# A recommendation tower on one core: the order in which TensorE turns the gathered embeddings is changed

## What is computed

```python
e = jnp.stack([tbl_0[ids[:, 0]], ..., tbl_26[ids[:, 26]]], axis=1)       # 2048 x 27 x 128
interactions = jnp.einsum('bfd,bgd->bfg', e, e)
flat_interactions = interactions[:, _TRIU_I, _TRIU_J]                     # 351 pairs, i < j
z = jnp.concatenate([e.reshape(B, -1), flat_interactions], axis=1)
h = jnp.concatenate([z, dense_ctx], axis=1)                               # 2048 x 3823
h = jnp.maximum(h @ W_top1 + b_top1, 0.0)                                 # 512
h = jnp.maximum(h @ W_top2 + b_top2, 0.0)                                 # 256
y = h @ W_top3
```

## Time and profile before

| | |
|---|---|
| median of three runs | 576.74 us |
| span of the profiled execution | 708.0 us |
| mean granted TensorE clock in it | 0.908 |
| PE busy | 574.9 us, 81% of the span |
| POOL busy | 416.2 us, 59% |
| DVE busy, ACT busy | 347.6 us, 232.3 us |

### The profile page before, as it was taken

How to read it: one execution, slowest core, us unless ns; L and a number is a source line. 1 busy time by engine, 2 the same in 40 slices (tenths; PEclk the granted TensorE clock), 3 DMA queues, 4 the chain that set the end, 5 groups by cost and what they waited for, 6 DMA issues and landing times.

```text
span 708.0 us, 7882 instructions
## 1 busy us (share of the span) xinstructions
PE 574.9 (81%) x2578; PEld 504.6 (71%) x2578; DVE 347.6 (49%) x1140; ACT 232.3 (33%) x703; POOL 416.2 (59%) x450
## 2 busy tenths in 40 slices
PE   2606688989889898959959896897968979698898
PEld 1505577868778787948848795786857868697786
DVE  4305462819264563808337281554707355372755
ACT  4204423324251513315232331514315161323441
POOL 6775565666666565665746667365664666556001
PEclk9956899989989998989989899799987999989999
DMA  6613411111111111111111111011110111111000
GB/s 211 217 52 110 131 45 44 46 46 44 45 45 50 41 49 41 48 45 39 47 29 50 44 42 52 27 49 42 46 52 26 49 41 49 42 41 46 12 1 1
DMA packets 19581, 37.84 MB, mean 53 GB/s; under 512 B 7780, under 2 KB 8804, under 8 KB 19540
## 3 DMA queue, kind: packets, MB, share of 16 engines
q0 software_dynamic: 13824, 28.34, 15.1%
q1 hardware_dynamic: 5716, 8.99, 4.0%
HBM read 37.30 MB, written 0.01 MB: 53 GB/s over the span
## 4 chain that ended last, share of the span: by engine, by line
PE 59%; another core or an unknown queue 20%; DVE 8%; issue 6%; ACT 5%; DMA 1%; SPq 0%; ACTq 0%; DVEq 0%
PE ps_acc L298 12%; PE ps_acc L299 11%; PE ps_acc L300 11%; PE ps_gram L323 10%; DVE g_buf L666 6%; PE ps_acc L356 6%; PE ps_t L269 5%; PE ps_gram L400 3%; ACT g_buf L582 2%; DVE emb_x L645 1%; DMA g_buf<-in_W_top 1%; ACT emb_x L534 1%; ACT h_t L571 1%; PE ps_gram L352 1%
## 5 line engine op out<-in xcount | busy, mean ns | idle before, releaser
L242 POOL DMA_INDIRECT emb<-in_tbl,idx x405 | 385.8, 953 | 233.4 <-issue 109.4
L298 PE MATMUL ps_acc<-w_hi,emb_x 128*128 128x512 f32 x432 | 211.1, 489 | 28.7 <-DVE emb_x L645 26.6
L645 DVE TENSOR_TENSOR emb_x<-ps_t,emb_x 128x512 fp32r<-128x512 f32 (+1 forms) x111 | 73.9, 667 | 249.6 <-ACT emb_x L534 165.2
L299 PE MATMUL ps_acc<-w_lo,emb_x 128*128 128x512 f32 x432 | 182.7, 423 | 0.0
L300 PE MATMUL ps_acc<-w_hi,emb_x 128*128 128x512 f32 x432 | 181.0, 419 | 0.0
L666 DVE COPY g_buf<-ps_gram 32x112 f32<-32x112 f32 x480 | 129.8, 270 | 93.6 <-PE ps_gram L323 63.1
L323 PE MATMUL ps_gram<-emb_x 128*128 128x224 f32 x480 | 99.5, 335 | 79.2 <-DVE emb_x L645 41.2
L298 PEld LDWEIGHTS ps_acc<-w_hi,emb_x 128*128 128x128 f32 x432 | 131.9, 305 | 35.3 <-DVE emb_x L645 28.0
L323 PEld LDWEIGHTS ps_gram<-emb_x 128*128 128x128 f32 x480 | 83.4, 231 | 102.0 <-DVE emb_x L645 45.1
L582 ACT ACTIVATE g_buf<-ps_gram 32x112 f32<-32x112 f32 x480 | 122.2, 255 | 99.0 <-PE ps_gram L323 64.8
L534 ACT ACTIVATE emb_x<-ps_t 128x512 fp32r<-128x512 f32 (+1 forms) x111 | 63.1, 583 | 272.7 <-PE ps_t L269 137.4
(11 more groups left out here) (61 smaller groups left out, 163.2 us busy)
## 6 DMA issues: line engine op xcount, KB each, us to landing
g_buf<-in_W_top SPq DMA_DIRECT2D x27, 256.0 KB
emb<-in_tbl,idx POOLq DMA_INDIRECT x405
w_cols<-in_W_top SPq DMA_DIRECT2D x1, 512.0 KB
w<-in_W_top SPq DMA_DIRECT2D x1, 512.0 KB
emb<-in_tbl,idx_first POOLq DMA_INDIRECT x27
w_cols<-in_W_top SPq DMA_DIRECT2D x1, 222.0 KB
idx<-in_ids SPq DMA_DIRECT2D x1, 216.0 KB, 4.9
ctx_rows<-in_dense_ctx SPq DMA_DIRECT2D x4, 32.0 KB
```

Source lines behind the costliest of these rows:

```text
L242: pool.indirect_dma_start(out=emb[:, f * D:(f + 1) * D], out_offset=None, in_=tables[f], in_offset=bass.IndirectOffsetOnAxis(ap=rows, axis ...
L298: pe.matmul(acc, emb_part(0, f), w_hi[:, f, :], start=(f == 0), stop=False)
L299: pe.matmul(acc, emb_part(0, f), w_lo[:, f, :], start=False, stop=False)
L645: dve.tensor_tensor(group_part(1, g), turned_bank(n, g), group_part(0, g).bitcast(fp32), ALU.subtract).then_inc(s_emb_lo, 1)
```

## The change

TensorE visits the turns in four places a tile. Groups 2 and 3 are turned one behind the other after the products of group 0; groups 4 and 5 together with the columns after those of group 2; group 6 behind the columns' product; h1 and groups 0 and 1 of the next tile behind unit 11. The two tables that were left for behind the second layer are now multiplied between the units. ScalarE's and VectorE's orders follow: ScalarE copies the columns behind group 5, relu and h1 stand later; VectorE makes the low part of the next tile's group 0 ahead of its last emptying, and that of group 1 ahead of the big transpose, and adds and packs in one piece behind group 3. The last tile's order is as before, but for its first two low parts.

```diff
--- before.py
+++ after.py
@@ -440,7 +440,7 @@
 
 
 
-            BEFORE_UNIT = [2, 0, 0, 2, 0, 0, 1, 0, 0, 1, 0, 0, 1, 0, 0, 0]
+            BEFORE_UNIT = [3, 0, 0, 2, 0, 0, 2, 0, 0, 2, 0, 0, 2, 0, 0, 0]
             assert len(BEFORE_UNIT) == UNITS and sum(BEFORE_UNIT) <= NF - 4 * GF
 
             pe.wait_ge(s_ident, 1)
@@ -449,35 +449,30 @@
             for t in range(TILES - 1):
                 multiply_group(t, 0)
                 turn_group(t, 2)
+                turn_group(t, 3)
                 multiply_group(t, 1)
-                turn_group(t, 3)
                 multiply_group(t, 2)
+                turn_group(t, 4)
+                turn_group(t, 5)
                 if t > 0:
                     turn_columns(t - 1)
-                turn_group(t, 4)
+                multiply_group(t, 3)
                 if t > 0:
                     multiply_columns(t - 1)
-                multiply_group(t, 3)
-                turn_group(t, 5)
-                if t > 0:
-                    turn_h1(t - 1)
+                turn_group(t, 6)
                 f = 4 * GF
-                for _ in range(GF if t == 0 else 2):
-                    multiply(t, f)
-                    f += 1
-                turn_group(t, 6)
                 for k in range(UNITS):
                     for _ in range(min(BEFORE_UNIT[k], NF - f)):
                         multiply(t, f)
                         f += 1
                     gram_unit(t, k)
-                    if k in (8, 14):
-                        turn_group(t + 1, (k - 8) // 6)
+                    if k == 11:
+                        if t > 0:
+                            turn_h1(t - 1)
+                        turn_group(t + 1, 0)
+                        turn_group(t + 1, 1)
                 if t > 0:
                     layer_2(t - 1)
-                while f < NF:
-                    multiply(t, f)
-                    f += 1
 
 
 
@@ -609,14 +604,14 @@
                         for c in GROUPS[g]:
                             split_weights(c)
                     split_group(t, g)
-                    if t > 0 and g == 3:
+                    if t > 0 and g == 5:
                         take_columns(t - 1)
-                    if t > 0 and g == 4:
+                    if t > 0 and g == 6:
                         relu_h1(t - 1)
-                    if t > 0 and g == 5:
-                        take_h1(t - 1)
                 for k in range(0, UNITS, 2):
                     take_blocks(t, k)
+                    if t > 0 and k == 10:
+                        take_h1(t - 1)
             t = TILES - 1
             for g in range(5):
                 split_group(t, g)
@@ -737,22 +732,22 @@
                     if t == 0:
                         for c in GROUPS[g]:
                             split_weights(c)
-                    split_group(t, g)
+                    if t == 0 or g > 1:
+                        split_group(t, g)
                     if t > 0:
-                        if g == 0:
+                        if g == 1:
                             turn_blocks(t - 1)
-                        if g == 1:
+                        if g == 3:
                             add_parts(t - 1)
-                            pack_pairs(t - 1, 0, 10)
-                        if g == 2:
-                            pack_pairs(t - 1, 10, NF - 1)
+                            pack_pairs(t - 1, 0, NF - 1)
                             if t > 1:
                                 layer_3(t - 2)
                 for k in range(1, UNITS, 2):
+                    if k == UNITS - 1:
+                        split_group(t + 1, 0)
                     take_blocks(t, k)
+                split_group(t + 1, 1)
             t = TILES - 1
-            split_group(t, 0)
-            split_group(t, 1)
             turn_blocks(t - 1)
             split_group(t, 2)
             layer_3(t - 2)
```

## The result

The changed kernel took 580.03 us (median of 4 runs, 579.27 to 581.5), the kernel before beside it 577.37 (4 runs): ratio 1.0057, 95% interval 1.0034 to 1.0079. It is slower by 0.6%; no change had been forecast.

The account below looks back on a forecast made before the run. TensorE was taken to bound the kernel, 34.13 us a tile, just ahead of GpSimd's 33.7. + 4.0 at the start, - 4.3 in 13 tiles and + 0.3 at the end gave 576.7 us, range 574 to 580 (8 in 10: 571 to 585).

Parts of the forecast that it names:

- The late signals: Kernel before's first profile: some 142 of 708 us are waits of an unknown queue, belonging to that execution only.
- whatever the others do: GpSimd's gathers: 27 x 1.249 = 33.7 us a tile, independent of the other engines.
- the check by which I came to 34.13: Kernel before: 75.2 to tile 1's units, 13 tiles of 34.0, 57.8 to the end: 575.0; median 576.74 gives 34.13.
- unit 15: TensorE waits for ScalarE to empty unit 12's bank: new wait of 0.95 us a tile.
- the first product: Next tile's first product waits for group 0's low part: new wait of 0.6 us.
- the columns' turn: TensorE waits for VectorE's queue, summed to end at 25.2, after turns 4 and 5 at 24.85: new wait 0.35 us.
- The start: Tile 1: group 5's early turn waits some 3 us for gathers; units start at 79.2, not 75.2, 4.0 us behind.
- It may not run faster than 33.7 a tile either: Changed kernel's tiles: the gathers' rate of 33.7 us is the floor, below the 33.8 forecast for TensorE.
- The end: From unit 0 of tile 14 to the last tile's first turn: + 0.3 us.
- The late start isn't regained: Slower rival: group 5's turn ahead of group 3 costs 4.0 us; 581, or 584 if tiles grow by 0.2; chance 0.22.
- The tiles gain more: Faster rival: tiles save more than forecast, 575.4 at the gathers' floor, 569.5 without it, together some 572; chance 0.26.
- The clock falls: Slower rival: twelve turns between unit 11 and the next product lower TensorE's clock; 587 to 609 us; chance 0.10.

Follow-up runs that it names:

- the second experiment: Both kernels without the product of high embeddings by low weights: kernel before 573.72 us, ratio 0.9934; changed kernel 579.81 us, ratio 1.0040.
- second profile: Trace of the kernel before, unchanged, run again without late signals: span 576.6 us; timed 577.11 us, ratio 0.9994.

## Why the prediction was wrong

**Where TensorE and the gathers stood.** Right in kind: TensorE's order sets the pace of the kernel before, in tiles of 33.94 (I used 34.13), and the gathers could go a little faster (33.72 where almost nothing holds them, by the second experiment; I had 33.7). The late signals did belong to the profiled execution. But the pace of the gathers was wrong: they don't run at their 33.7 "whatever the others do" even here, but come at 33.94, held here and there by VectorE, and TensorE doesn't notice. And three errors of the check by which I came to 34.13 cancelled out, which was luck: tile 1's units come at 80.54, not 75.2; a tile is 0.19 shorter, 2.5 us in 13; and the end from tile 14 on is 54.8, not 57.8, which I had read from the disturbed trace.

**The tile's own work.** I took 33.8 for TensorE in the new order. Alone it needs 33.3 (without the addition) to 33.45 (group 5 late). The waits were smaller than I had them: unit 15 0.70, not 0.95; the first product 0.30, not 0.6; the columns' turn nothing but 0.24 in the last tile, not 0.35 each (the pieces of that sum add up to 25.07, not the 25.2 written, so 0.2 by its own terms). Two stood at the places that the prediction named, and the size was off to the good side.

**The start.** This step failed: "Units of tile 1 then start at 79.2 instead of 75.2. The change begins 4.0 us behind." The changed kernel's 79.43 was nearly as forecast, but the other kernel isn't ahead there. TensorE of the kernel before, second profile:

```profile
49.41 1.12 PE L269 MATMUL ps_t<-ident,emb 128*128 128x128 f32 x4 [2.11 <-DMA emb<-in_tbl,idx]
...
58.34 0.61 PE L298 MATMUL ps_acc<-w_hi,emb_x 128*128 128x512 f32 x1 [1.94 <-DVE emb_x L645]
...
71.85 0.94 POOL L242 DMA_INDIRECT emb<-in_tbl,idx  x1 [0.30 <-issue]
...
78.70 0.49 PE L269 MATMUL ps_t<-ident,emb 128*128 128x128 f32 x3
...
80.54 0.71 PE L323 MATMUL ps_gram<-emb_x 128*128 128x224 f32 x5
```

The turn of group 1 waits for its gathers at the end of tile 0, the first product for its low part, and then 22.2 us pass without a wait for gathers. Tile 1 takes TensorE's own time behind a late beginning. Its last gather starts at 71.85, near the 71.3 that I had, but TensorE turns group 6 at 78.70, not 2 us behind it. I had worked out when the last gather lands and not asked when TensorE would be there. In the changed kernel:

```profile
53.26 0.66 PE L269 MATMUL ps_t<-ident,emb 128*128 128x128 f32 x4 [2.47 <-DMA emb<-in_tbl,idx]
...
59.23 0.80 PE L298 MATMUL ps_acc<-w_hi,emb_x 128*128 128x512 f32 x1 [1.95 <-DVE emb_x L640]
...
79.43 0.82 PE L323 MATMUL ps_gram<-emb_x 128*128 128x224 f32 x6
```

it begins 0.9 later and is at its units 1.1 earlier (from trace to trace this moment varies by more than that, so the 1.1 is no gain). The experiment with only group 5 early, 80.34, shows the same: there is no step of 4.0. Nor did the turn of group 5 wait 3 us in tile 1. It begins at 70.61 without a wait, and waits 0.5 to 1.0 us in each of the tiles 2 to 14 instead.

**The tiles.** This is the step that decided. "It may not run faster than 33.7 a tile either": the term was mis-sized. In the changed kernel the gathers take 34.13, because each tile has a gather under the addition that takes some 0.4 us more: 33.72 + 0.41. Without the addition the held gathers go, and the time with them (575.43): this much is shown.

Why the addition meets a gather in every tile isn't shown. I read it as a ring: TensorE waits for group 5's gathers, all that follows keeps a fixed distance from that wait, the next tile's addition too, and so the addition meets the gather at the same point in every tile. The held gather begins 0.31 to 0.47 us behind the addition's start in 12 of 15 tiles, which fits, but the ring was not tried apart, and it can't be all. With group 5 turned late the gathers came at 34.1 though TensorE waited for none of them from 54 to 381 us. And the kernel before without a product waits for gathers in every tile, yet its addition holds one gather in 15 tiles. What counts is where the addition falls: in the kernel before, it mostly falls where it holds nothing or 0.1; the early turn of group 5 alone was enough to put it on a gather of 1.55 to 1.70 us in ten tiles.

I wrote 27 x 1.249 "whatever the others do", with the 1558 ns of the longest gather in the same row, and didn't look at what stood beside it: it began at 421.84 under the packing (line 702, 421.23 to 422.58) and ended 0.82 behind its end. So TensorE's tile fell by 0.5 us, more than the 0.33 forecast, and the gathers' tile rose by 0.4 above the floor and past the old 33.94.

The Trainium skill (SBUF — State Buffer, the box on the trap "DVE blocks DMA") states that GpSimd can't write the descriptors of its DMAs while VectorE runs an operation in a two-port mode, which locks GpSimd out of the port pair that they share. It names a copy from SBUF to SBUF as one. The trace agrees in kind, that a gather begun under some VectorE operations is held; but here the holders are operations with two operands in SBUF, the addition first. The Trainium skill (SBUF — State Buffer, section "A bandwidth-pool intuition that's wrong") gives "DVE-end + ~115 ns" for a DMA under a copy. This trace shows another figure for GpSimd's instruction: the gather ends 0.82 us behind.

**The end.** +1.4, not +0.3. From unit 0 of tile 14 to the first turn that stands in the last tile (group 2) it is 14.3 us (523.34 to 537.67) against 13.4 (521.73 to 535.13), with 0.70 ahead of unit 15 and 0.30 ahead of this turn among it. The columns' turn in the last tile comes another 0.4 later:

```profile
547.32 0.60 PE L269 MATMUL ps_t<-ident,emb 128*128 128x128 f32 x4
548.15 0.55 PE L352 MATMUL ps_gram<-ident,cols 128*128 128x128 f32 x3 [0.24 <-DVE cols L697]
```

against, in the kernel before:

```profile
544.75 0.60 PE L269 MATMUL ps_t<-ident,emb 128*128 128x128 f32 x4
545.19 0.49 PE L352 MATMUL ps_gram<-ident,cols 128*128 128x128 f32 x3
```

From unit 0 of tile 14 to the end it is 55.8 us in both traces of the changed kernel without the addition, so some 0.5 of the 1.4 goes with the addition. The rest is read from the two traces alone; no kernel was run to test it.

**The rivals.** "The late start isn't regained" gave 581 and the right side, and named the right place, the turn of group 5 ahead of group 3. The agreement of its 581 with 580.03 is luck, for its mechanism is not the one: the price isn't paid once at the start but by 0.2 us in each tile. "The tiles gain more" was right of TensorE's own order and met the gathers' floor, which lay higher than its 33.7. "The clock falls" didn't come about: the granted clock was 1.00 around the twelve turns in a row.

## What to carry to other kernels

Where two engines stand within one per cent of each other, work out for each what it is held by, and not only its own rate: a new order of one also moves how their instructions lie beside each other, and a collision that was rare, or small, can become one per round. A transfer's longest duration in the view of its line is a question to follow up before its median is multiplied. And a start is as late as the latest of all that it needs, so ask of the waiting engine too when it would have been there.

## What the runs showed of the hardware

- A gather (indirect DMA of 128 rows issued by GpSimd) takes 0.944 us of GpSimd. One that begins under VectorE's fp32 addition of two SBUF operands (128x729, 0.90 us) ends 0.81 to 0.82 us behind the addition's end, in each of the 15 tiles of the changed kernel. One that began before the addition is not stretched (0.95 us at most in all traces).
- What holds a gather has two operands in SBUF. Over the 18 traces of this case, of the gathers begun under the weights' subtraction (0.69 us) 117 of 251 took more than 1.0 us, under the last layer's work (line 717, 0.43 us) 44 of 68 (up to 1.18). Of those begun under the low part, whose one operand is in PSUM (874), under the copies that empty the units (1914), and under the transpose from SBUF to SBUF (3.7 us; 776), none took more than 0.96.
- A row of short additions can hold like a long one: the packing, up to 26 of them back to back, made 34 of the 471 gathers begun under it longer than 1.0 us, one of them 2.02 us. Of 13 gathers begun under the addition in four pieces (1.12 us in sum), 5 were held until 0.82 us behind the last piece, 8 got through earlier.
- Of two additions of 0.90 us one behind the other, it was the first alone that held the gather in 24 of 30 tiles. Two in place of one cost nothing that can be measured in either kernel.
